# Quantisation on GpSimd, a reordered cross attention, one norm for two, and a swapped pair on VectorE

## The reference

```python
x = x + tanh(g_xattn[0]) * L0_xattn(norm(x), ctx, mask)   # 16 heads of 8
x = x + tanh(g_ffn[0])   * L0_ffn(norm(x))                # 16 experts
x = x + tanh(g_xattn[1]) * L1_xattn(norm(x), ctx, ctx)    # one head, sigmoid gate
x = x + tanh(g_ffn[1])   * L1_ffn(norm(x))                # quantised weights + lora, gelu
x = x + tanh(g_xattn[2]) * L2_xattn(ctx, norm(x))         # 8 heads of 64, own layernorms
x = x + tanh(g_ffn[2])   * L2_ffn(norm(x))                # 8 experts
x = x + tanh(g_xattn[3]) * L3_xattn(norm(x), ctx, ctx)    # 16 heads of 8
x = x + tanh(g_ffn[3])   * L3_ffn(norm(x))                # 64 experts

def fake_quant_weight(w):            # of L1_ffn, for W_fc and W_proj
    scale = max(abs(w)) / 127
    wq = clip(round(w / scale), -128, 127) * scale
    return w + (wq - w)

def L2_xattn(ctx, latents):          # latents = norm(x)
    xn = layernorm(ctx) * m_w + m_b
    ln = layernorm(latents) * l_w + l_b
    q, kv = ln @ Wq, concat([xn, ln]) @ Wkv
    ...
```

## Time and profile before

| what | value |
| --- | --- |
| median of 3 runs | 680.71 us (679.11 to 683.18) |
| the profiled execution | 680.45 us, span 678.3 us |
| mean granted TensorE clock | 0.957 |
| TensorE busy | 613.6 us, 90% of the span |
| TensorE weight loads | 411.4 us |
| VectorE busy | 397.2 us |
| ScalarE busy | 385.9 us |
| GpSimd busy | 195.1 us |

### The profile page before, as it was taken

How to read it: one execution, slowest core, us unless ns; L and a number is a source line. 1 busy time by engine, 2 the same in 40 slices (tenths; PEclk the granted TensorE clock), 3 DMA queues, 4 the chain that set the end, 5 groups by cost and what they waited for, 6 DMA issues and landing times.

```text
span 678.3 us, 10957 instructions
## 1 busy us (share of the span) xinstructions
PE 613.6 (90%) x3608; PEld 411.4 (61%) x3608; DVE 397.2 (59%) x750; ACT 385.9 (57%) x759; POOL 195.1 (29%) x189
## 2 busy tenths in 40 slices
PE   9999986899699997888797998899986899999997
PEld 6467764676554444666453444467654678878885
DVE  2278838567642446666226565378859465565665
ACT  4477864555445335888653444477872555656653
POOL 4000022770000000000000344000022677787775
PEclk9999979899679999999979999899987899999999
DMA  8100001110000000000000001000000122211110
GB/s 286 65 1 2 2 15 33 31 48 1 0 1 0 0 1 0 1 3 1 1 0 0 25 23 61 1 3 1 2 32 16 31 63 62 62 47 49 59 31 32
DMA packets 9611, 18.57 MB, mean 27 GB/s; under 512 B 1856, under 2 KB 3024, under 8 KB 9440
## 3 DMA queue, kind: packets, MB, share of 16 engines
q1 hardware_dynamic: 9568, 18.01, 8.5%
HBM read 17.48 MB, written 0.52 MB: 27 GB/s over the span
## 4 chain that ended last, share of the span: by engine, by line
PE 81%; DVE 8%; issue 5%; ACT 4%; POOL 1%; ACTq 0%; DVEq 0%; POOLq 0%
PE bank L647 8%; PE bank L648 8%; PE bank L649 8%; PE bank L564 4%; PE bank L575 4%; PE bank L894 3%; PE bank L590 3%; PE bank L526 3%; PE bank L489 3%; PE bank L664 3%; PE bank L908 2%; PE bank L538 2%; PE bank L883 2%; PE bank L1004 2%; PE bank L860 2%
## 5 line engine op out<-in xcount | busy, mean ns | idle before, releaser
L402 POOL TENSOR_TENSOR h_lo<-wc,h_hi 128x512 fp32r<-128x512 f32 x82 | 105.9, 1293 | 75.1 <-ACT h_hi L1232 74.7
L1224 ACT ACTIVATE wa<-bank 128x512 f32<-128x512 f32 x84 | 50.3, 599 | 85.5 <-PE bank L649 85.5
L1636 DVE TENSOR_TENSOR wb<-wa,bank 128x512 f32<-128x512 f32 x80 | 54.8, 688 | 67.5 <-PE bank L649 52.4
L647 PE MATMUL bank<-xn_hi,w_hi 128*128 128x512 f32 x168 | 69.0, 411 | 10.8 <-DVE wc L1628 6.1
L648 PE MATMUL bank<-xn_lo,w_hi 128*128 128x512 f32 x168 | 66.9, 398 | 0.0
L649 PE MATMUL bank<-xn_hi,w_lo 128*128 128x512 f32 x168 | 66.7, 397 | 0.0
L1643 DVE TENSOR_TENSOR wc<-wb,bank 128x512 f32<-128x512 f32 x80 | 54.8, 687 | 10.2 <-PE bank L664 5.8
L1232 ACT ACTIVATE h_hi<-wc 128x512 fp32r<-128x512 f32 x84 | 52.3, 624 | 13.0 <-DVE wc L1628 4.9
L1445 DVE TENSOR_REDUCE row_max<-bank 128x4 f32<-128x512 f32 x64 | 43.6, 682 | 20.3 <-PE bank L564 19.6
L430 POOL TENSOR_TENSOR x<-x,upd 128x128 f32 x16 | 7.3, 455 | 150.7 <-ACT upd L1101 150.7
L1449 DVE TENSOR_TENSOR wa<-bank,row_max 128x512 f32<-128x512 f32 x64 | 44.3, 692 | 7.6 <-ACT wb L1114 4.4
(11 more groups left out here) (270 smaller groups left out, 1273.1 us busy)
## 6 DMA issues: line engine op xcount, KB each, us to landing
ring<-in_experts SPq DMA_DIRECT2D x42, 256.0 KB, 2.6
ring<-in_experts SPq DMA_DIRECT2D x8, 192.0 KB, 2.5
mats<-in_mats SPq DMA_DIRECT2D x1, 1472.0 KB, 10.1
mats<-in_mats SPq DMA_DIRECT2D x1, 832.0 KB, 6.2
mats<-in_mats SPq DMA_DIRECT2D x2, 320.0 KB, 8.2
x<-in_x_t SPq DMA_DIRECT2D x1, 512.0 KB, 4.0
context<-in_ctx_t SPq DMA_DIRECT2D x1, 512.0 KB, 4.8
select<-in_select SPq DMA_DIRECT2D x1, 512.0 KB, 11.2
```

The source lines that it names most:

```text
L402: nc.gpsimd.tensor_tensor(h_lo[:, k % 2, :], wc[:, k % 2, :], h_hi[:, k % 2, :].bitcast(f32), ALU.subtract).then_inc(m_h_lo, 1)
L647: mm(out, w, x_, start=start, stop=False)
L1224: fn(wa[:, k % 2, :], bank[k % 2][:, :], ACT.Silu).then_inc(m_silu, 1)
L1636: v.tensor_tensor(wb[:, par, :], wa[:, par, :], bank[2 + par][:, :], ALU.mult).then_inc(m_t, 1)
```

## The change

1. The maxima of the weights, the reduction over partitions and the scale's three small steps stand before the first attention. GpSimd does the quantisation in 20 steps (ten for each matrix, since a step with two operations on two tensors becomes two), three behind each of the first six updates and two behind the seventh, with `diag` as scratch. The loop over batches is written out.
2. In the first cross attention the scores come ahead of values and gate, the lora products ahead of the centring, the output product ahead of the variances; the tables of ScalarE follow (Exp, Sigmoid, Sqrt), and the update stands ahead of the context's roots. VectorE adds lora right behind the softmax.
3. Layer 2's two norms become one: sqrt(var * (1 + eps) + eps^2).
4. In the second cross attention VectorE normalises unit n ahead of the maximum of unit n+2.

```diff
@@ -168,10 +168,12 @@
         NORM_OF = {}
         for s in range(8):
             NORM_OF[s] = [len(NORMS)]
-            NORMS.append((whole(x), whole(xn), None, ("x", s)))
             if s == 4:
-                NORM_OF[s].append(len(NORMS))
-                NORMS.append((whole(xn), latent_half(1), (LNLW, LNLB), ("xn", s)))
+                NORMS.append((whole(x), latent_half(1), (LNLW, LNLB), ("x", s)))
+            else:
+                NORMS.append((whole(x), whole(xn), None, ("x", s)))
...
+        eps_col, eps2_col = sb("eps_col", [P, 1]), sb("eps2_col", [P, 1])
+        w_scale, w_inv, w_neg = w_stat[:, 0:2], w_stat[:, 2:4], w_stat[:, 4:6]
+        d_scaled, d_step = signal("d_scaled"), signal("d_step")
+        QUANTISED = 20
+
+        def ffn_weights(n):
+            return mats1[:, (5 + 4 * n) * P:(9 + 4 * n) * P]
...
+            quantised = [0]
+
+            def step(ins):
+                quantised[0] += 1
+                ins.then_inc(d_step, 1)
+                pool.wait_ge(d_step, quantised[0])
...
+            def fake_quantise(n, k):
...
+                w = ffn_weights(n)
+                s1, i1_, n1 = w_scale[:, n:n + 1], w_inv[:, n:n + 1], w_neg[:, n:n + 1]
+                q, e = diag[:, 0, :], diag[:, 1, :]
+                if k == 0:
+                    if n == 0:
+                        pool.wait_ge(d_scaled, 1)
+                    step(nc.gpsimd.tensor_scalar(q, w, i1_, None, ALU.mult))
+                if k == 1:
+                    step(nc.gpsimd.tensor_scalar(e, q, n1, None, ALU.mult))
+                if k == 2:
+                    step(nc.gpsimd.tensor_tensor(e, e, w, ALU.add))
+                if k == 3:
+                    step(nc.gpsimd.tensor_scalar(e, e, i1_, None, ALU.mult))
+                if k == 4:
+                    step(nc.gpsimd.tensor_tensor(q, e, q, ALU.add))
+                if k == 5:
+                    step(nc.gpsimd.tensor_scalar(q, q, ROUND, ROUND, ALU.add, ALU.subtract))
+                if k == 6:
+                    step(nc.gpsimd.tensor_scalar(q, q, 127.0, -128.0, ALU.min, ALU.max))
+                if k == 7:
+                    step(nc.gpsimd.tensor_scalar(e, q, s1, None, ALU.mult))
+                if k == 8:
+                    step(nc.gpsimd.tensor_tensor(e, e, w, ALU.subtract))
+                if k == 9:
+                    step(nc.gpsimd.tensor_tensor(w, w, e, ALU.add))
...
 
-            attn(0)
+            pool.wait_ge(d_rowmax, 2)
+            nc.gpsimd.partition_all_reduce(w_max[:, 2:4], w_max[:, 0:2], P, REDUCE_MAX).then_inc(d_max, 1)
+            for b in range(B):
+                pool.wait_ge(update_ready, b + 1)
+                dst = x[:, b // BH, b % BH * P:b % BH * P + P]
+                nc.gpsimd.tensor_tensor(dst, dst, upd[:, 0:P], ALU.add).then_inc(x_updated, 1)
+                for k in range(3 * b, min(3 * b + 3, QUANTISED)):
+                    fake_quantise(k // 10, k % 10)
             pool.wait_ge(in_mats3, 16)
...
             moe(MOE[0])
-            pool.wait_ge(d_rowmax, 2)
-            nc.gpsimd.partition_all_reduce(w_max[:, 2:4], w_max[:, 0:2], P, REDUCE_MAX).then_inc(d_max, 1)
...
                 pe.wait_ge(ln_out, 2 * NORM_OF[2][0] + c + 1)
                 mm(bank[2 + c][:, :], w[:, 0:P], xn[:, c, :], start=True, stop=True).then_inc(b_proj, 1)
-            for c in range(2):
-                pe.wait_ge(b_evac, c + 1)
-                mm(bank[6 + c][:, :], w[:, 3 * P:4 * P], xn[:, c, :], start=True, stop=True)\
-                    .then_inc(b_proj, 1)
...
                 last.then_inc(b_s, 1)
             for c in range(2):
+                for j in range(BH):
+                    last = mm(bank[4 + c][:, j * P:j * P + P], context[:, c, j * P:j * P + P],
+                              w[:, 2 * P:3 * P], start=True, stop=True)
+                last.then_inc(b_v, 1)
+            for c in range(2):
+                mm(bank[6 + c][:, :], w[:, 3 * P:4 * P], xn[:, c, :], start=True, stop=True)\
+                    .then_inc(b_proj, 1)
+            pe.wait_ge(b_p, 1)
+            mm(bank[0][:, :], lora[:, 0:P], lora[:, P:5 * P], start=True, stop=True).then_inc(d_lora, 1)
+            pe.wait_ge(b_p, 2)
+            for j in range(4):
+                last = mm(bank[1][:, j * P:j * P + P], lora[:, 5 * P + j * P:5 * P + j * P + P],
+                          lora[:, 9 * P:10 * P], start=True, stop=True)
+            last.then_inc(d_lora, 1)
+            for c in range(2):
                 mm(bank[2 + c][:, :], centre[:, :], context[:, c, :], start=True, stop=True).then_inc(xc_centred, 1)
...
             pe.wait_ge(in_consts, 64)
-            i0, i2 = NORM_OF[4]
-            norm(i0)
-            norm(i2)
+            i4 = NORM_OF[4][0]
...
-                    fn(rstd[:, c, :], bank[2 + c][:, 0:BH], ACT.Sqrt, bias=eps_col[:, :])\
-                        .then_inc(ln_std, 1)
+                    twice = i == NORM_OF[4][0]
+                    fn(rstd[:, c, :], bank[2 + c][:, 0:BH], ACT.Sqrt, bias=(eps2_col if twice else eps_col)[:, :],
+                       scale=1.0 + EPS if twice else 1.0).then_inc(ln_std, 1)
...
             norm(NORM_OF[2][0])
-            nc.scalar.preload_act_table(ACT.Sigmoid)
+            nc.scalar.preload_act_table(ACT.Exp)
...
             for c in range(2):
+                act.wait_ge(b_p, c + 1)
+                fn(wb[:, c, :], wa[:, c, :], ACT.Exp).then_inc(b_e, 1)
+            nc.scalar.preload_act_table(ACT.Sigmoid)
+            for c in range(2):
                 act.wait_ge(b_proj, 5 + c)
                 fn(gate1[:, c, :], bank[6 + c][:, :], ACT.Sigmoid, bias=col(G1B)).then_inc(b_evac, 1)
+                act.wait_ge(b_tr, c + 1)
+                fn(wc[:, c, :], bank[4 + c][:, :], ACT.Copy).then_inc(b_pt, 1)
             for c in range(2):
                 act.wait_ge(xc_centred, c + 1)
                 fn(ctx_sq[:, c, :], bank[2 + c][:, :], ACT.Square).then_inc(xc_sq, 1)
                 fn(ctx_cen[:, c, :], bank[2 + c][:, :], ACT.Copy).then_inc(xc_cen, 1)
-            for c in range(2):
-                act.wait_ge(b_p, c + 1)
-                fn(wb[:, c, :], wa[:, c, :], ACT.Exp).then_inc(b_e, 1)
             nc.scalar.preload_act_table(ACT.Sqrt)
             for c in range(2):
-                act.wait_ge(b_tr, c + 1)
-                fn(wc[:, c, :], bank[4 + c][:, :], ACT.Copy).then_inc(b_pt, 1)
+                act.wait_ge(b_y, c + 1)
+                update(2, bank[c][:, :], x_count(1, 1) + c, HALF)
             for c in range(2):
                 act.wait_ge(xc_var, c + 1)
                 fn(rstd_ctx[:, c, :], bank[4 + c][:, 0:BH], ACT.Sqrt, bias=eps_col[:, :]).then_inc(xc_std, 1)
-            for c in range(2):
-                act.wait_ge(b_y, c + 1)
-                update(2, bank[c][:, :], x_count(1, 1) + c, HALF)
...
-            for i in NORM_OF[4]:
-                norm(i)
+            norm(NORM_OF[4][0])
...
                 for n in range(4 * B):
+                    normalise(n)
                     if n + 2 < 4 * B:
                         largest(n + 2)
-                    normalise(n)
...
+            dve.wait_ge(in_mats1, 32)
+            for n in range(2):
+                v.tensor_reduce(w_max[:, n:n + 1], ffn_weights(n), X, ALU.max, apply_absolute_value=True)\
+                    .then_inc(d_rowmax, 1)
+            dve.wait_ge(d_max, 1)
+            link(v.tensor_scalar(w_scale, w_max[:, 2:4], 1.0 / 127.0, None, ALU.mult))
+            link(v.reciprocal(w_inv, w_scale))
+            v.tensor_scalar(w_neg, w_scale, -1.0, None, ALU.mult).then_inc(d_scaled, 1)
             attn(0)
...
-            def largest_weights():
...
-            def quantisation_steps():
...
-            def fake_quantise(n):
-
-                w = mats1[:, (5 + 4 * n) * P:(9 + 4 * n) * P]
-                s1, i1_, n1 = scale[:, n:n + 1], inv[:, n:n + 1], neg[:, n:n + 1]
-                q, e = sq[:, 0, :], sq[:, 1, :]
-                link(v.tensor_scalar(q, w, i1_, None, ALU.mult))
-                link(v.scalar_tensor_tensor(e, q, n1, w, ALU.mult, ALU.add))
-                link(v.scalar_tensor_tensor(q, e, i1_, q, ALU.mult, ALU.add))
-                link(v.tensor_scalar(q, q, ROUND, ROUND, ALU.add, ALU.subtract))
-                link(v.tensor_scalar(q, q, 127.0, -128.0, ALU.min, ALU.max))
-                link(v.scalar_tensor_tensor(e, q, s1, w, ALU.mult, ALU.subtract))
-                link(v.tensor_tensor(w, w, e, ALU.add))
-
-
-            dve.wait_ge(in_mats1, 32)
-            largest_weights()
             norm(NORM_OF[2][0])
-            quantisation_steps()
...
-            fake_quantise(0)
...
             for c in range(2):
+                dve.wait_ge(b_v, c + 1)
+                v.tensor_copy(v1[:, BH * c:BH * c + BH, :], bank[4 + c][:, :]).then_inc(b_vev, 1)
...
                     .then_inc(b_n, 1)
-            fake_quantise(1)
+            dve.wait_ge(d_step, QUANTISED)
+            for n in range(2):
+                dve.wait_ge(d_lora, n + 1)
```

(11 more changed lines are left out.)

57 lines of the change are left out of this document (17 added, 40 removed).

## The result

The changed kernel took 664.0 us in the median of its first four runs (660.49 to 665.78), the kernel before 679.96 in the median of four beside it; the ratio is 0.9766, with a 95% interval from 0.9734 to 0.9798. Two later sets of runs of the same kernel gave 0.9706 [0.9657, 0.9755] and 0.9746 [0.9705, 0.9788]. It is faster by 2.3 to 2.9%, some 16 to 20 us, where 21.8 were forecast: inside the range of 653 to 667 each time. Of the three medians (664.0, 661.64, 663.38) one lies in the 655 to 662 that the likeliest case gave itself, two just above. The profiled execution took 662.29 us, with a span of 660.5. Medians are over all runs of a set; ratios and their intervals leave out the few runs that were over 1.5% longer than the fastest of the same kernel.

The account below looks back on a forecast made before the run. It took TensorE being held up or slowed (late softmax, table load, queue order, norms, batch waits, half clock) as the bound. 9.7 + 0.5 - 0.1 + 0.1 + 5.3 + 6.3 = 21.8 us off 680.45 gave 658.7, median 659.0; range 653 to 667.

Parts of the forecast that it names:

- the likeliest case: Whole kernel: the main forecast of 659.0 us, with its own range of 655 to 662 and chance 0.63.
- First cross attention, reordered: First cross attention: scores ahead of values and gate, lora ahead of transposes; second sum done at 181.1, gain 9.7 us.
- The walk: First cross attention: new queues followed step by step with the old profile's durations, from scores at 163.7 to 181.1.
- The 0.5 behind it: Stretch from the first cross attention's sums to the next product: VectorE's two lora sums gone, gain 0.5 us.
- that this stretch keeps its clock losses I assume: Up products behind the first cross attention: clock losses stay; upper bound if the clock stayed whole, 1.7 us more.
- Quantisation on GpSimd: First attention: 20 GpSimd steps, 19.6 us in all, fit its idle time; cost 0.1 us, ends 0 and 1.0.
- the blocking rival: First attention: GpSimd's steps and VectorE block each other, costing 34 us, total 693 us; chance 0.03.
- Maxima ahead of the first attention: Before the first attention: weight maxima, reduction and small steps finish before the scores; cost 0, other end 2 us.
- One norm: Ahead of the second cross attention: one norm for two, first product 5.9 us earlier, 0.6 lost to half clock; gain 5.3.
- Second cross attention: Second cross attention: normalising before the later maximum cuts batches from 8.63 to 7.7 us; gain 6.3 us.
- The swapped wait: Second cross attention, rival: the later maximum delays the exponential of n+2, swapping one wait for another; 665.3 us, chance 0.11.
- the clock takes part of it back: Rival: TensorE falls to 1.2 GHz after idle spells, with little to do from 178 to 184; 3 to 5 us, chance 0.12.

Follow-up runs that it names:

- the third profile: The changed kernel run unchanged a third time, in one set with the second cheaper-steps run and the fill in three norms: median 663.38 us.
- the moved load: Changed kernel with ScalarE's Sqrt load put behind both first cross attention updates and the norm's squares, VectorE's context-norm reciprocals moved likewise: 660.72 us, ratio 0.9676.
- the order alone: Changed kernel with two norms and the old maximum-before-normalisation order again, keeping the first cross attention's order and GpSimd's quantisation: 680.29 us, ratio 0.9952.

## Why the prediction was right, and where it was off

- **First cross attention, reordered, 9.7: right, 9.2.** The walk came out within a microsecond at each step: output products at 176.4 (175.7), the Sqrt load at 177.23 ahead of the update as forecast, second sum over at 181.6 (181.1). The 0.5 behind it measured 0.3 (9.55 at the up products). The step "that this stretch keeps its clock losses I assume" was wrong: the up products came at full clock, and 1.7 us more were ahead at 202 (11.24), just the 1.7 of the upper bound.
- **Quantisation on GpSimd, -0.1: right in effect.** The last update of the first attention came 0.3 us later (92.12, before 91.83), the norm behind it 0.05 later; from first to last update it is 41.9 us, before 41.2. The term mis-sized is the price of one-input steps, 0.77 us from the row of an instruction with two operations; with one they take 1.57, the rounding 1.95. The place that became tight was the sixth batch, not the seventh: its three steps ran from 84.64 to 88.94 and held the seventh update to 89.03 (before 88.66). VectorE's maxima kept 682 ns, its subtractions 691 (692), so the blocking rival (693 us) fell. The rule of the Trainium skill, GPSIMD Engine Reference, section on elementwise cycle accounting, that two-input arithmetic takes about twice VectorE's time, held (1.27 beside 0.69).
- That quantisation mattered in the walk at all was the wrong weight: taken out of the old order it gains nothing, put back in the new one it costs 1.8 us. So the order and the tables carry 7.4 of the 9.2 by themselves, and the move to GpSimd adds 1.8 only together with them.
- **Maxima ahead of the first attention, 0: right.** The first score's maximum stood at 31.21, before at 31.22.
- **One norm, 5.3: right, 5.2** in the full change (11.2 to 16.4), 4.7 alone. The half clock behind it was there (0.62).
- **Second cross attention, 6.3: right, 6.3** (16.4 to 22.65), and 6.3 alone. The swapped wait fell.
- **The sum's hidden step**: durations from one profile, so the clock's losses elsewhere were taken as fixed. They aren't. Of the 11.2 us gained in the first cross attention and behind it, up to 7 us were clock (5.3 if the 0.65 over 15.1 us of the earlier trace rows is made whole, 1.7 in the up products), and the changed kernel paid 6.8 in the last attention. The rival "the clock takes part of it back" (662 to 664, chance 0.12) fits the profiled 662.3 and the medians best, and deserved more; its place (178 to 184) was wrong, its price of 3 to 5 us is near what is missing in the end (1.8 to 5.8 us under the 21.8). In sum the changed kernel is ahead by 22.65 at 312; then come 2.7 more by clock until 345 and 0.6 more until 401, 6.8 are lost in the last attention and about 1.4 over the rest, which leaves 17.8. That the total lay so well in the range is in part luck: clock gains that were not forecast (1.7 and 2.7) stood against clock losses that were not either.

That the last attention's length goes with its clock is shown by all profiles: 26.6 to 27.2 us at 1.00, 28.1 to 28.4 at 0.94, 30.95 at 0.83, 35.1 to 35.2 at 0.71, with the same work (but for dummies). That is the measured cost of the clock there. That filling keeps the clock whole there is shown twice. The 6.8 us lost there in the changed kernel are no fixed price of the change: code that is the same up to that stage lost 5.7 us ahead of it instead, and the third profile lost 2.6 us in it (30.95 beside 28.35). What stays open is why a run takes one course or the other: the profiles show no edit that decides it.

## What to carry to other kernels

Price a change stage by stage, and check it there by landmarks that both kernels have; the total adds several microseconds of clock, from which the gain of one part can't be told (9.2 us in its stage, 3.3 in the total). Before crediting an edit with relieving an engine, ask what else holds the chain: here the table loads and the place in TensorE's queue did. Where many short idle moments of TensorE precede a dense stretch, a handful of dummy products in them is a cheap trial. Set it beside a profile that came to that stage with the same low stretches, and look at what follows as well: here 1.3 of 1.75 us went again in one case.

## What the runs showed of the hardware

- A stretch in which TensorE was busy for 13.70 of 13.70 us ran at a granted clock of 0.50 throughout, in four profiles (the changed kernel twice, the moved load, the order alone). Ahead of it, from 398 to 417 in the changed kernel, stood idle moments of 0.8 to 1.4 us each, none longer. With such moments filled, two profiles ran this stage at 1.00, where twelve without filling had 3.4 us or more at half clock; neither of the two had arrived as those four did.
- Two kernels whose instructions stood within 0.03 us of each other from 160 to 202 were given 3.4 and 6.8 us at half clock from the same moment, 206.9, on. One and the same code up to 398 showed both courses: 3.4 us there, then none until 343; or 6.8 us there, then 3.4 at 253 and 6.8 at 321. The first course took 241.2 us from the norm ahead of the first cross attention to that of the last attention, the second 246.9. Low stretches came again at the same places in profiles of one kernel, within half a microsecond in one pair.
- GpSimd multiplies 128x512 values by a column in 1.57 us with one operation in the instruction, in 0.69 with two, the second changing nothing. Adding and subtracting a constant takes 1.95, taking minimum and maximum 0.61.
- GpSimd's sum of 128x128 took 0.80 us in the second cross attention beside 0.46 in the first, with and without the change: in the first, 27.9 us of GpSimd's work left VectorE's maxima at 682 ns and its subtractions at 691 (before 692).
